# Key-tile sum of the probabilities: GpSimd additions replaced by a row of accumulating transfers in SBUF

## The reference

```python
# 1: attention over the 1024 positions, queries and keys from the context
q = einsum('dc,bct->btd', Wq, ctx) + bq
k = einsum('dc,bct->bdt', Wk, ctx) + bk
attention = softmax(einsum('btd,bds->bts', q, k), axis=-1)    # 1024 x 1024
v = einsum('oc,bct->bto', Wv, norm(x)) + bv
x = x + einsum('bts,bsc->bct', attention, v)
# 2: sign weights with routed scales in and out
x = x + (norm(x) * in_scale) @ sign(weight).T * out_scale + bias
# 3: attention of the 128 rows of x on the 128 rows of the context
# 4: eight low-rank experts of rank 16, weighted by a router
```

## Time and profile before

| | |
|---|---|
| median of three runs | 2435.04 us |
| the profiled execution | 2432.91 us |
| its span, first to last instruction | 2431.1 us |
| granted TensorE clock, mean | 0.982 |
| PE busy | 2207.9 us (91%) |
| DVE busy | 1835.1 us (75%) |
| ACT busy | 1108.3 us (46%) |
| POOL busy | 822.2 us (34%) |
| DMA | 115.58 MB, mean 48 GB/s |
| one turn of the loop | 68.39 us, 32 turns with attend |

### The profile page before, as it was taken

One profiled execution on the slowest core, in us unless ns is written; L12 is line 12 of the kernel. 1 busy time (PEld: TensorE's weight loads), 2 busy tenths in 40 slices (PEclk: granted clock), 3 DMA queues, 4 the chain that ended last, 5 costly groups with the idle time before them and its releaser, 6 DMA issues.

```text
span 2431.1 us, 34048 instructions
## 1 busy us (share of the span) xinstructions
PE 2207.9 (91%) x11102; PEld 1704.5 (70%) x11102; DVE 1835.1 (75%) x2906; ACT 1108.3 (46%) x1593; POOL 822.2 (34%) x520
## 2 busy tenths in 40 slices
PE   1998999999999999999999999999999999999986
PEld 1775777777777777777777777777777777777764
DVE  2336778887878878887878878787878878787873
ACT  2004444445554444445554444445554544445541
POOL 0003433334434433334434433334434433334430
PEclk7999999999999999999999999999999999999996
DMA  8001011111111111111111111111111111111100
GB/s 231 10 10 56 31 44 52 35 52 52 44 42 52 43 43 52 35 52 52 43 43 52 43 43 52 35 52 52 43 43 52 43 43 52 35 52 52 42 20 26
DMA packets 50217, 115.58 MB, mean 48 GB/s; under 512 B 14800, under 2 KB 23248, under 8 KB 50192
## 3 DMA queue, kind: packets, MB, share of 16 engines
q1 hardware_dynamic: 38624, 113.26, 14.2%
q10 hardware_dynamic: 11568, 1.98, 0.5%
HBM read 81.67 MB, written 16.78 MB: 40 GB/s over the span
## 4 chain that ended last, share of the span: by engine, by line
PE 61%; DVE 13%; issue 10%; ACT 6%; POOL 1%; DVEq 0%; DMA 0%; ACTq 0%; POOLq 0%; SPq 0%
PE acc L1030 9%; PE acc L1069 8%; DVE p_lo L888 7%; PE scores L1013 5%; PE shared L993 5%; PE acc L1026 2%; PE acc L1027 2%; PE acc L1028 2%; PE shared L1196 2%; PE shared L1138 2%; PE shared L1154 2%; PE shared L1086 2%; PE scores L1165 2%; PE scores L999 2%; PE scores L1159 2%
## 5 line engine op out<-in xcount | busy, mean ns | idle before, releaser
L624 POOL TENSOR_TENSOR p_sum<-p_sum,prob 128x1024 f32<-128x1024 f32 x192 | 494.4, 2575 | 125.7 <-ACT prob L688 119.9
L888 DVE TENSOR_TENSOR p_lo<-prob,p_hi 128x1024 fp32r<-128x1024 f32 x256 | 451.7, 1781 | 99.9 <-ACT p_hi L695 89.5
L781 DVE TENSOR_REDUCE neg_max<-scores 128x1 f32<-128x1024 f32 x256 | 312.5, 1221 | 63.6 <-PE scores L1013 58.2
L605 POOL TENSOR_TENSOR rstd<-var_eps,minus_half 128x1 f32<-128x1 f32 x128 | 126.8, 991 | 666.2 <-DVE var_eps L775 661.9
L688 ACT ACTIVATE prob<-scores 128x1024 f32<-128x1024 f32 x256 | 260.5, 1017 | 197.0 <-PE scores L1058 178.0
L695 ACT ACTIVATE p_hi<-prob 128x1024 fp32r<-128x1024 f32 x256 | 271.4, 1060 | 75.6 <-PE acc L1069 71.5
L621 POOL TENSOR_TENSOR p_sum<-prob 128x1024 f32<-128x1024 f32 x32 | 85.6, 2676 | 630.7 <-ACT prob L688 630.7
L1030 PE MATMUL acc<-m_whole,cT_whole 128*128 128x512 f32 x512 | 255.2, 600 | 0.0
L1069 PE MATMUL acc<-p_hi,v_hi 128*128 128x512 f32 x512 | 175.5, 424 | 76.9 <-DVE p_lo L888 76.7
L1013 PE MATMUL scores<-k_hh,q_hl 128*128 128x512 f32 x512 | 211.7, 494 | 0.3 <-issue 0.3
L1043 PE MATMUL shared<-signT,y_hi 128*128 128x512 f32 x512 | 207.0, 404 | 0.4 <-ACT oscale L677 0.4
(11 more groups left out here) (215 smaller groups left out, 4535.4 us busy)
## 6 DMA issues: line engine op xcount, KB each, us to landing
c_in<-in_ctx SPq DMA_DIRECT2D x32, 512.0 KB, 3.3
xn<-in_x SPq DMA_DIRECT2D x32, 512.0 KB, 4.2
x<-in_x SPq DMA_DIRECT2D x32, 512.0 KB, 3.3
c_val<-in_ctx SPq DMA_DIRECT2D x32, 512.0 KB, 3.6
out_x<-oscale SPq DMA_DIRECT2D x32, 512.0 KB, 2.9
q_m<-q_hl SPq DMA_DIRECT2D x32, 256.0 KB, 3.1
k_hh<-k_hh SPq DMA_DIRECT2D x32, 256.0 KB, 3.5
wq_nat<-in_L_xattn_Wq SPq DMA_DIRECT2D x4, 1024.0 KB, 10.0
```

Of the source, the lines that this page charges most:

```text
L624: nc.gpsimd.tensor_tensor(p_sum[:, :], p_sum[:, :], prob[s % 2][:, :], ALU.add).then_inc(p_summed, 1)
L781: nc.vector.tensor_reduce(neg_max[:, t:t + 1], scores[t % 2][:, :], AX_X, ALU.max, negate=True).then_inc(row_max, 1)
L888: nc.vector.tensor_tensor(p_lo[s % 2][:, :], prob[s % 2][:, :], p_hi[s % 2][:, :].bitcast(F32), ALU.subtract).then_inc(p_lo_ready, 1)
```

## The change

The seven additions by GpSimd become eight transfers within SBUF, issued by GpSimd in a row. The first copies tile 0 into `p_sum`. Each of the other seven adds its tile to `p_sum` in the transfer (`accum_op=ALU.add`). Before each issue POOL waits for the exponential of the tile and for the completion of the transfer before it; then it runs a [128, 1] multiplication into a new tile `turn` and issues. `p_summed` now counts 16 for each transfer, 128 a batch. The exponential of tile s waits for the transfer of tile s-2, as before it waited for the addition of that tile.

```diff
-                        if attend and s >= 1:
+                        if attend:
+                            pool.wait_ge(turned, nth(8, a, s))
                             pool.wait_ge(exp_ready, nth(8, a, s + 1))
-                            if s == 1:
+                            if s == 0:
                                 pool.wait_ge(xnT_done[1], nth(2, c, 2))
                                 pool.wait_ge(den_done, nth(1, a - 1, 1))
-                                nc.gpsimd.tensor_tensor(p_sum[:, :], prob[0][:, :], prob[1][:, :], ALU.add).then_inc(p_summed, 1)
+                                nc.gpsimd.tensor_tensor(turn[:, :], minus_half[:, :], minus_half[:, :], ALU.mult).then_inc(turned, 1)
+                                pool.dma_start(p_sum[:, :], prob[0][:, :]).then_inc(p_summed, 16)
                             else:
-                                pool.wait_ge(p_summed, nth(7, a, s - 1))
-                                nc.gpsimd.tensor_tensor(p_sum[:, :], p_sum[:, :], prob[s % 2][:, :], ALU.add).then_inc(p_summed, 1)
+                                pool.wait_ge(p_summed, nth(128, a, 16 * s))
+                                nc.gpsimd.tensor_tensor(turn[:, :], minus_half[:, :], minus_half[:, :], ALU.mult).then_inc(turned, 1)
+                                pool.dma_start(p_sum[:, :], prob[s % 2][:, :], accum_op=ALU.add).then_inc(p_summed, 16)
...
-                            act.wait_ge(p_summed, nth(7, a, (-1, 0, 1)[s] if s < 3 else s - 2))
+                            act.wait_ge(p_summed, nth(128, a, 16 * (s - 1)))
                             nc.scalar.activation(prob[s % 2][:, :], scores[s % 2][:, :], ACT.Exp).then_inc(exp_ready, 1)
...
-                            pe.wait_ge(p_summed, nth(7, a, 7))
+                            pe.wait_ge(p_summed, nth(128, a, 128))
                             pe.wait_ge(exp_ready, nth(8, a, 8))
```

More of the change, by code:

```diff
@@ L426, in build @@
         r_bias = sb("r_bias", [P, 1])
+        turn = sb("turn", [P, 1])
         r_exp = [sb(f"r_exp{i}", [P, E]) for i in range(2)]
@@ L505, in build @@
         p_summed = sem("p_summed")
+        turned = sem("turned")
         den_inv_ready = sem("den_inv_ready")
```

## The result

The changed kernel takes 2851.72 us (median of 4 runs, 2846.22 to 2861.97) against 2435.5 us before: ratio 1.1716, 95% interval [1.1681, 1.175]. The forecast was 3000 us, in a range of 2580 to 3450.

What follows compares the result with a forecast made beforehand. PE was taken as the bound, made to wait for the chain: 47.0 - 31.0 + 1.7 = 17.7 us more in 31 turns, 20.3 in turn 1, together 569 us on 2432.9, so 3000 us; range 2580 to 3450.

Steps and rivals of the forecast that it cites:

- A: Stretch from the first exponential's end to the denominators: 30.96 us before the change, forecast to last the chain's 47.0 us.
- The chain's length: First exponential to finished sum: copy 4.5 plus seven adding links of 5.7 us, 44.4; 47.0 with shared DMA engines.
- the rival with the short link: POOL's issue costs nothing extra: copy 3.5, adding link 4.7, chain 36.4 us; 2610 us, 2665 with clock loss; chance 0.20.
- The second read: In each adding transfer `p_sum` is read besides `prob`: 2 x 1.3 = 2.5 us of data at 416 GB/s.
- Sharing: Loads, `q_m` and `k_hh` use the same DMA engines for 6.0 us; 44%, 2.6 us, is added to the chain.
- The clock: PE idles some 9 us before the sum, its clock falls: 1.7 us lost in each of 31 turns.
- B: Stretch from the denominators to the next batch's first exponential's end: 37.43 us before, forecast 1.7 us longer.
- the likeliest range: Whole kernel at 2750 to 3200 us, with links of 5 to 6.3 us; chance 0.47, giving 3000 us.
- The signs: Landings 4 to 5.5 us, `p_lo` 1.2, PE's wait before denominators 11 to 14, turn 86, clock falling behind it.
- The gain: PE's `p_lo` stalls in the tile loop vanish: at most 76.7 us, 2.4 a turn, swallowed by the chain.
- The point of decision: Link length of 3.6 us, under which the chain ends before PE arrives and the transfers are hidden.
- The rival that ends faster: Links under 3.6 us hide the transfers and `p_lo` takes 1.21 us: 2356 us; chance 0.04.

Runs made afterwards that it cites:

- e1: The changed kernel with all eight transfers as plain copies, the sum over tiles left out: 2474.29 us, ratio 1.0164.
- e2: The changed kernel with the seven adding transfers taking only half of each tile, the other half's sum left out: 2648.83 us, ratio 1.0877.
- e3: The changed kernel with SP issuing `q_m` and `k_hh` only after the eighth `p_sum` transfer has landed: 2817.54 us, ratio 1.1571.
- e4: The changed kernel with 30 filler matmuls on constant data where PE waits for the sum: 2825.22 us, ratio 1.158.
- e7: The changed kernel with `q_m` and `k_hh` issued after the last `p_sum` landing and 28 filler matmuls in PE's wait: 2740.93 us, ratio 1.1258.
- e5: The changed kernel with only the copy of tile 0 left, the seven adding transfers and their waits left out: 2329.9 us, ratio 0.9562.
- e9: Against the changed kernel: tiles 0 to 5 in two rows of three transfers, then three GpSimd additions, complete sum: 2432.41 us, ratio 0.9988.

## Why the prediction was right

- *The bound.* PE would have to wait for the row of links, and the work behind it would follow. Both hold: copies in place of additions (e1) take A from 40.0 to 29.9 us.
- *The chain's length, 47.0 us forecast, 40.0 measured.* This is the term that was mis-sized most. An adding link was set at 5.7 us and is 4.7, the copy at 4.5 and is about 3.1. The 1.0 us for POOL's issue was too much. POOL's instruction takes 0.85 us, but the landing of 4.5 us counts from its start: 2.1 fixed and 2.4 of data, with nothing on top. This was the rival with the short link. Eight times 1.0 us, and 0.4 of the copy, are 8.4 us too much. The prediction's other estimate, a link of 4.4 us and a chain of 34 us, was nearer to the 36.0 of the links alone than its own sum of 44.4.
- *The second read.* Doubling the time of the data for an addition was right: 2.9, 3.3 and 4.5 us in e1, e2 and the changed kernel; that it is a read stays argued. Of the rates measured before, 416 GB/s was the right choice and 251 the wrong one; e1's copies over 128 partitions land faster than the loads.
- *Sharing, 2.6 us forecast.* Links alone come to 3.1 + 7 x 4.7 = 36.0 us. The rest of A, 4.0 us, is sharing and the slower `turn` steps. e3 took 1.0 us of it away. In the turn that starts at 1438.66, of the quicker kind with an A of 38.8 us, two `turn` steps of 0.67 and 1.12 us instead of 0.19, with the issues behind them, make 1.4 us. The second transfer, with `c_in` and `xn` issued beside it, lands 0.5 us late there, and the last two are 0.3 and 0.2 us late. So sharing is some 2 us of the 2.6 forecast, and the slow steps were missing in the forecast.
- *The clock, 1.7 us forecast, 3.8 measured.* This term was too small by more than half. The price came from a turn in which the clock was down for less of the work than here: 0.77 and 0.80 over 8 us, against 0.50 over the 8 us behind 1397. e4 and e7 show that these 3.8 us are the clock's: B returns to 37.5 us where PE does not wait.
- *The sum.* 17.7 us a turn were forecast and 12.9 measured: 7.0 too much in A, 2.1 too little in B.
- *Luck.* The time lies in the likeliest range, 2750 to 3200 us, but the links that this range stood for, 5 to 6.3 us, did not occur. The link is that of the short rival, whose price was 2610 us, or 2665 with the clock. That rival was priced without sharing and with the clock at 1.7 us; with what was measured it is the result: 36.0 + 4.0 - 30.9 + 3.8 = 12.9 us a turn. So errors against each other keep the forecast as near as 5%.
- *The signs.* Landings of 4.5 us, line 893 at 1.22 us and the clock behind the denominators came as forecast. The wait before the denominators is 6.3 us and not 11 to 14, and a turn 81.2 us and not 86. The chain was shorter, and PE now waits 2.4 us of it earlier, at line 1151, by way of ACT. The prediction looked at ACT's norm there and not at the softmax of sublayer 3.
- *The gain.* `p_lo` at 1.22 us throughout came true and was swallowed, as forecast. Its worth without the chain is 106 us (e5), not 77. Of this 7 us are turn 1's, whose A fell from 26.7 to 19.8 us; the rest is 3.1 us a turn, and the waits of PE at one line were less than what the additions cost.
- *The point of decision.* The rival that ends faster asked for links under 3.6 us. e1 has them (2.9 us to landing), and it was still slower than before. Eight links of 3.1 us would be 25 us, but late issues and sharing made the row 29.9 us, with its end 1.8 us after PE was ready. The rule "shorter than PE's work" was too kind, as it left out both these and the clock.

## What to carry to other kernels

A row of dependent transfers costs its landing times, not its bytes alone: multiply the landing of one (here about 2 us, and the tile's bytes at some 430 GB/s, counted twice for an addition) by the number of links, add what other transfers and late issues cost, and compare with the work of the engine that waits at the end, before the additions are moved off an engine. Two overlapping rows of three transfers, with three additions by GpSimd behind them, did what eight in a row could not; rows of four and three with two additions were still 5.8% slower than before. When TensorE waits even a short time ahead of small matmuls, look at the granted clock behind the wait, since the loss there can exceed the wait (1.6 us for 0.4 in e9). A few filler matmuls cut to the wait's length got it back here, and too many cost their own time.

## What the runs showed of the hardware that I had not expected

- The clock fell in e9's turns with a wait of only 0.38 us before the denominators, in about two turns of three, and cost 1.6 us. Stalls of 0.73 and 1.16 us in the tile loop of the kernel before left it at 1.00. What stands behind the wait in e9 are 16 small matmul records. The wait was 0.37 to 0.40 us in the turns that kept the clock as well as in those that lost it, so its length alone does not decide; what does is open.
- A transfer issued within 0.5 us of an adding one slows it by more than its own bytes. A half addition beside the load of `x` landed 2.6 us later (e2), where 512 KB are 1.3 us at 416 GB/s; in the few turns of e2 with `x` issued 2.6 us or more behind it, it landed in time. A whole addition beside `q_m` and `k_hh` landed 2.6 us later, while `q_m` issued 0.8 us or more behind it cost 0.3. Why was not tried.
- A transfer issued by GpSimd lands no later than those issued by SP: 2.9 us for 512 KB within SBUF in e1, against 3.3 us for SP's `c_in` and 2.9 us for its store `out_x` of that size. These go from and to HBM, so the issuing engine alone was not compared. The Trainium skill ("DMA: Bandwidth & Descriptors", section "Anatomy of one DMA") gives 2.0 us + bytes / 436 GB/s, 3.2 us here; the measured 2.9 is a little under it, and its 2.0 us fixed agree with the 2.1 of the adding transfers from e2 and the changed kernel.
- The cost of GpSimd's additions to the turn was 3.1 us, nearly a third more than TensorE's waits for the delayed `p_lo` show.
- An adding transfer kept the DMA engines busy for 2.8 us, a copy of the same tile for 1.4 us, while the page counts the same bytes for both.
